# A DLRM tower on one core: GpSimd's two signals per tile at the first and the fifth eighth of the gram

## The reference

```python
e = jnp.stack([tbl_0[ids[:, 0]], ..., tbl_25[ids[:, 25]]], axis=1)
all_vecs = jnp.concatenate([dense_proj[:, None, :], sparse_embs], axis=1)
interactions = jnp.einsum('bnd,bmd->bnm', all_vecs, all_vecs)
interact_flat = interactions[:, rows, cols]
z = jnp.concatenate([dense_proj, interact_flat], axis=1)
h = jnp.concatenate([z, r_dense_proj], axis=1)
h = jnp.maximum(h @ W_top1 + b_top1, 0.0)
h = jnp.maximum(h @ W_top2 + b_top2, 0.0)
y = h @ W_top3
```

## Time and profile before

| | |
|---|---|
| median of 3 runs | 486.37 us (485.76 to 494.1) |
| the profiled execution | 485.11 us, of which the span is 483.2 |
| TensorE, matmuls | 382.4 us busy, 79% |
| TensorE, weight loads | 353.0 us, 73% |
| GpSimd | 254.9 us, 53% |
| VectorE | 230.3 us, 48% |
| ScalarE | 144.2 us, 30% |
| mean granted TensorE clock | 0.898 |

### The profile page before, as it was taken

How to read it: one execution, slowest core, us unless ns; L and a number is a source line. 1 busy time by engine, 2 the same in 40 slices (tenths; PEclk the granted TensorE clock), 3 DMA queues, 4 the chain that set the end, 5 groups by cost and what they waited for, 6 DMA issues and landing times.

```text
span 483.2 us, 14444 instructions
## 1 busy us (share of the span) xinstructions
PE 382.4 (79%) x6144; PEld 353.0 (73%) x6144; DVE 230.3 (48%) x702; ACT 144.2 (30%) x256; POOL 254.9 (53%) x260
## 2 busy tenths in 40 slices
PE   0756439686788988798799888888988899897977
PEld 0746329676777988587698887788877798786866
DVE  4779428446433375334565456446554545431110
ACT  1156013131322235024141425133324225142422
POOL 6067744655664556556666555655555766553000
PEclk9979859788898879899989988998899979897899
DMA  6998912323141422517242332313131311100000
GB/s 118 230 242 147 264 48 44 85 53 87 48 95 40 51 78 48 82 38 77 75 68 68 51 86 53 82 46 95 43 92 43 97 45 49 38 27 27 4 3 0
DMA packets 25766, 35.86 MB, mean 74 GB/s; under 512 B 6605, under 2 KB 19789, under 8 KB 25743
## 3 DMA queue, kind: packets, MB, share of 16 engines
q1 hardware_dynamic: 16399, 18.72, 20.4%
q0 software_dynamic: 8192, 16.79, 12.0%
q10 hardware_dynamic: 1152, 0.01, 0.1%
HBM read 35.49 MB, written 0.01 MB: 73 GB/s over the span
## 4 chain that ended last, share of the span: by engine, by line
PE 75%; issue 16%; DMA 5%; SPq 2%; POOL 1%; ACT 0%; DVE 0%; POOLq 0%
PE gram L424 12%; PE hid L395 11%; PE look_ps L351 7%; PE vec_act L312 7%; PE look_ps L353 7%; PE look_odd L351 6%; PE look_odd L353 6%; PE hid L402 5%; PE hid L351 4%; PE hid L353 4%; DMA raw<-tbl 3%; PE small L414 2%; DMA vecs<-tbl,ids_sb 2%; POOL vecs L295 1%; PE small L364 1%
## 5 line engine op out<-in xcount | busy, mean ns | idle before, releaser
L295 POOL DMA_INDIRECT vecs<-tbl,ids_sb x256 | 254.7, 995 | 184.5 <-issue 101.0
L572 DVE TENSOR_SCALAR onehot<-step_ids,row_no 125x256 fp32r<-125x256 int32 x640 | 187.9, 364 | 180.1 <-remote 84.4
L424 PE MATMUL gram<-vecs_T 128*27 128x26 f32 x4096 | 61.8, 201 | 52.1 <-issue 51.9
L424 PEld LDWEIGHTS gram<-vecs_T 128*27 128x27 f32 x4096 | 51.5, 113 | 64.7 <-issue 60.6
L547 ACT COPY vecs_T<-vec_act 128x512 f32<-128x512 f32 x64 | 46.1, 728 | 148.1 <-PE vec_act L312 79.3
L351 PE MATMUL look_ps<-onehot,look_hi 125*128 125x256 f32 x256 | 74.0, 319 | 6.7 <-DVE look_lo L580 4.6
L351 PE MATMUL look_odd<-onehot,look_hi 125*128 125x256 f32 x256 | 69.2, 306 | 4.3 <-DVE look_lo L580 2.7
L353 PE MATMUL look_ps<-onehot,look_lo 125*128 125x256 f32 x256 | 69.3, 301 | 2.7 <-issue 2.7
L353 PE MATMUL look_odd<-onehot,look_lo 125*128 125x256 f32 x256 | 64.4, 287 | 0.0
L351 PEld LDWEIGHTS look_ps<-onehot,look_hi 125*128 125x128 f32 x256 | 53.5, 209 | 9.0 <-DVE look_lo L580 4.8
L351 PE MATMUL hid<-onehot,look_hi 125*128 125x256 f32 x128 | 42.6, 355 | 21.0 <-DMA ident<-identity 15.6
(11 more groups left out here) (74 smaller groups left out, 293.3 us busy)
## 6 DMA issues: line engine op xcount, KB each, us to landing
step_ids<-look_ids SPq DMA_DIRECT2D x15, 640.0 KB
raw<-tbl SPq DMA_DIRECT2D x10, 448.0 KB
vecs<-tbl,ids_sb POOLq DMA_INDIRECT x256
vecs<-dense SPq DMA_DIRECT2D x16, 64.0 KB
raw<-tbl SPq DMA_DIRECT2D x10, 52.0 KB
step_ids<-look_ids SPq DMA_DIRECT2D x1, 512.0 KB
w_sb<-w SPq DMA_DIRECT2D x1, 512.0 KB
raw<-w_dense SPq DMA_DIRECT2D x1, 512.0 KB
```

The source lines that it names most:

```text
L295: nc.gpsimd.indirect_dma_start(out=vecs[j][:, 1 + k, :], out_offset=None, in_=tables[k], in_offset=bass.IndirectOffsetOnAxis(ap=ids_sb[:, ...
L424: last = nc.tensor.matmul(gram[s * QUAD:s * QUAD + VECS, g, 0:2 * FOLD], v[:, 0:VECS], v.rearrange("d (h n) -> d h n", h=2)[:, :, 0:FOLD], ...
L572: last = nc.vector.tensor_scalar(onehot[:, i % SLOTS, c, :], step_ids[a][0:LOOK_K, f - a * LOOKUPS // 2, :], row_no[0:LOOK_K, ch:ch + 1], ...
```

## The change

```diff
-PARTS = 4
+PARTS = 8
 GRAM_PARTS = tuple(QUAD * n // PARTS for n in range(PARTS + 1))
...
                     wait_for_vecs(t, j, pair)
                     gram_part(j, 0).then_inc(gram_half0, 1)
-                    gram_part(j, 1)
+                    for part in range(1, PARTS // 2):
+                        gram_part(j, part)
 
                 def gram_second(j):
-                    gram_part(j, 2).then_inc(gram_half1, 1)
-                    gram_part(j, 3).then_inc(gram_ready, 1)
+                    gram_part(j, PARTS // 2).then_inc(gram_half1, 1)
+                    for part in range(PARTS // 2 + 1, PARTS - 1):
+                        gram_part(j, part)
+                    gram_part(j, PARTS - 1).then_inc(gram_ready, 1)
```

## The result

The changed kernel takes 522.45 us, median of 4 runs (515.07 to 528.09), beside 490.24 for 4 runs of the kernel before (485.76 to 495.51): a ratio of 1.0655, interval 1.0404 to 1.0906. The prediction was 486.0 with a range of 477 to 498. The profiled execution took 520.7 us, its span is 518.8, 35.6 us longer than before. Ratios here leave disturbed executions out and so aren't always the quotient of the two medians.

What follows compares the result with a forecast made beforehand. TensorE's gram and GpSimd's gathers were taken to hold each other in a ring paced by the gathers. From the profiled 485.1 us, -7.0 and +6.7 gave 484.8, as a time 486, with a range of 477 to 498.

Steps and rivals of the forecast that it cites:

- What bounds the kernel: TensorE's gram halves and GpSimd's gather sets hold each other up; gathers set the pace, TensorE's own turn some 10.5 us.
- Term 1: Gram signals come 32 records earlier, saving 0.28 us on each of 25 turns: 7.0 us off.
- The sign that I asked for: GpSimd's pause between gather sets in the settled turns: 2.8 us where it was 3.1.
- Term 2: Start-up gram half near 83 us: signal passes while GpSimd still gathers, TensorE stands through eight more gathers; 6.7 us lost.
- sixteen gathers on end: Expected mark of a too early signal: two gather sets without pause at 1.25 us, beside a gram half over 10 us.
- With 96 left it is 0.83, still inside: Gram records left after the signal take 0.83 us, within the 1.1 us GpSimd needs to its first gather.
- In the settled turns I expect none: Where 4 to 11 gram records pass among gathers, no signal was expected to release GpSimd before its set ends.
- None reached 64: In the profile before, no releasing gram half that met gathers let 64 records through before TensorE's release.
- A: Rival: no signal passes too early in any gram half, only the 7.0 us gain is left, 479 us; chance 0.24.
- C: Rival: TensorE's own work sets the pace in most turns, so the gain is hidden, 486 us; chance 0.08.
- B: Rival: in two or more gram halves the 32nd record passes while GpSimd gathers; +9.0 us, 495 us; chance 0.30.
- D: Rival: the change doesn't do what it says; excluded by the diff, the signal being on another matmul of the same sequence.

Runs made afterwards that it cites:

- one write: Changed kernel plus one GpSimd write, which GpSimd waits for, between signal and first gather: 490.55 us on a slower chip, ratio 1.0134 to the kernel before.
- three tiny writes: Changed kernel plus three small GpSimd scratch writes between each wait and the first gather: 516.94 us on a slower chip.
- kernel before, second trace: The unchanged kernel, one more execution with its trace, on a slower chip: 501.91 us.
- three eighths: Kernel before with both signals moved later, to 96 MATMUL records into each gram half: 487.2 us on a slower chip.
- 48 or 80 records: Kernel before with both signals moved to 48 or 80 MATMUL records into the half; quicker chips: 395.92, 396.99, 396.54 us and 397.27, 399.21 us.

## Why the prediction was wrong

**What bounds the kernel.** Right. The gathers halt TensorE (without them all but four halts in the gram are gone), it goes free 2.3 to 2.7 us after the last one's start, and its own turn is 10.2 us in the mean.

**Term 1, -7.0 us.** The signal does come 0.28 us earlier, in the clean half: the first gather is 0.18 us after the last record, where it was 0.45. But the gain never shows. It holds only as long as TensorE halts inside the gram, with nothing but gram records between its release and the signal; in 14 of 27 halves that is now not so, and sets begin 14.9 us apart in the mean, where it was 13.5 and not the 12.6 to come. The sign that I asked for was there: in 12 of the 13 halves with halts GpSimd's pause is 2.5 to 3.1 us, its median 2.7. But it says nothing of the other 14, where the pause is 4.4 to 11.9.

**Term 2, the step that failed.** It priced a signal that comes too early against GpSimd's *running* set, and looked for sixteen gathers on end. There is not one such place in the changed kernel's trace. In the half at 115.41, where 34 records went through at once, I should have seen one:

```profile
115.41 0.53 PE L424 MATMUL gram<-vecs_T 128*27 128x26 f32 x34
...
121.42 1.24 PE L424 MATMUL gram<-vecs_T 128*27 128x26 f32 x84 [0.51 <-issue]
```

GpSimd's timeline there:

```profile
118.94 0.94 POOL L295 DMA_INDIRECT vecs<-tbl,ids_sb  x1 [0.30 <-issue]
122.36 0.94 POOL L295 DMA_INDIRECT vecs<-tbl,ids_sb  x1 [2.47 <-issue]
```

GpSimd waited all the same, since the signal's semaphore rose only 6.16 us after the half began, when the gathers were over: this signal, raised among gathers, was held up with the rest. The loss came from the other side of the signal, the *next* set. The sentence that failed is "With 96 left it is 0.83, still inside": I took it that a first gather behind the last gram record is harmless however near. Counted over the releasing halves (a matmul of the gram or of a layer, two records, as one instruction), TensorE gets this many instructions from the gram's last record to its first halt:

| first gather after the last gram record | instructions |
|---|---|
| -0.37 to 0 us (changed kernel) | 19 to 29 |
| 0.17 to 0.19 us (changed kernel) | 25 to 47 |
| 0.16 to 0.26 us (one write) | 40 to 53 |
| 0.32 us (three tiny writes) | 47 to 55 |
| 0.27 to 0.29 us (kernel before, second trace) | 49 to 56 |
| 0.27 to 0.45 us (kernel before) | 53 to 63, once 29, once 51 |
| 0.35 to 1.41 us (one write) | 51 to 60 |
| 0.65 to 0.74 us (three eighths) | 56 to 61 |

Left out are one set of the kernel before at -0.83 us and all sets with a long gather or a long pause near their start, 11 of 27 in the changed kernel; there it is 60 to 73 wherever the first one starts, as if it had started later. It is a slope and not a step: some 25 at 0 us, near 60 from 0.45 on, with a scatter of ten or more between. The kernel before stands near its top, and the change moved the gathers down it. Between two halves of the gram in the loop lie 56 or, every fourth time, 60 such instructions. With 57 to 60 let through the first halt falls into the gram, just; with 25 to 47 it falls ahead of it. "In the settled turns I expect none" was wrong for the same reason: I read the settled turns for what slips into the gram, not for how little lies between their first halt and the gram's start. The trace of before had it: 4 to 11 records of 128 were through the earlier trace rows, a margin of a few instructions. And it had one set that began too early. "None reached 64" is wrong for the half at 140.01: 90 of its 128 records come before its last run. TensorE's timeline, and GpSimd's:

```profile
143.50 0.51 PE L424 MATMUL gram<-vecs_T 128*27 128x26 f32 x38 [1.11 <-issue]
```

```profile
142.99 1.06 POOL L295 DMA_INDIRECT vecs<-tbl,ids_sb  x1 [2.77 <-issue]
```

The set begins 0.83 us ahead of the last gram record, only some 30 instructions get through before the first halt, and the next half comes at 159.31, 19.3 us after this one. That was the changed kernel's loss, once, in the trace that the prediction was made from.

**Rivals.** A and C (479, 486) fell with term 1. B had the right sign and the wrong mechanism and size: 9 or 17 us by slips, none of which occurred on the slower chip, where 32 came. D isn't the case. The runs of the kernel before at 494.1 us, which I read as a hint of a slip, fit the edge seen in its second trace.

**Size.** The range ended at 498 because each loss was priced as one event. What happened is a changed turn in over half of the sets, +56.8 us between the halves against -23.5 in them.

## What to carry to other kernels

Where TensorE halts while GpSimd issues gathers, ask not how much idle time a line shows but what stands between the end of the halts and the next signal; here halts that fell into the block which raises the signal were cheap, and halts ahead of it delayed the whole ring. Count how many instructions lie between the last free moment and that block, and how many get through: a margin of a few is an edge, and a signal "earlier by 0.28 us" can fall off it. And time such a change on more than one chip: it was 6.5 and 7.6% in two measurements on slower ones, and nothing on a quicker one.

## What the runs showed of the hardware

**Semaphores arrive late, not only instructions.** From the start of the gram's last matmul to the rise of `gram_ready` it is 0.22 us (median) in the kernel before, over 1 us in one of 16 tiles (in two of the 13 that its second trace has). In the changed kernel the median is 1.9 us, the longest 7.1, and 11 of 16 are over 1 us (11 again in its second trace); with three eighths 0.24 and none, with one write 0.24 and two, without gathers 0.22 and none. The chain's new 6% of "another core or an unknown queue" may go with it. But late signals aren't what the loss is made of: with the first half's signal alone at the eighth one of 16 is late, with three tiny writes two, and both traces are over 520 us long; with the second half's alone it is 13. After the half at 115.41, whose last record starts at 122.4, VectorE's timeline has

```profile
129.50 1.05 DVE L557 STREAM_TRANSPOSE gram_rows<-gram 128x832 f32<-128x832 f32 x1 [12.00 <-remote]
```

and ScalarE's

```profile
133.84 1.32 ACT L550 COPY vecs_T<-vec_act 128x512 f32<-128x512 f32 x2 [17.32 <-remote]
```

the first 7 us after the gram was done. "Remote" is what the profile says where it finds no instruction that ended near the semaphore's rise. Copies of the transposes are late in both kernels; in the changed one it reaches `gram_ready` as well.

**A clock step follows the halts.** After the half at 190.85 to 197.4, which had halts, the changed kernel's window reads

```profile
197.80:200.30 2.50, 2.50 (x13) 2.50 (x13) 0.00 (x0) 0.00 (x0) 1.89 (x3) 0.50 0.36 60
```

a granted clock of 0.50, the 1.2 GHz level, with look-ups 0.21 us apart in place of 0.12. This is part of the 7 us that the lower clock makes of the loss.

**Plain loads didn't halt TensorE like that.** In one execution on the quicker chip 16 of them a tile, 0.55 us each, leave 23 of 27 halves at the 1.1 us of an undisturbed one; in the changed kernel's trace there, with gathers, it is 10. On a slower chip they weren't tried. The Trainium skill, "Runtime: NRT & Kernel Launch", section "Instruction fetch mechanics", has refills of instructions mostly hidden. With gathers the traces of the slower chips show matmul starts 0.7 and 1.4 us apart where the halts are, in code that runs without halts when no gathers are issued, except for the four longer ones named above. So whatever the refills cost, gathers decide it here; whether the four are refills, no run shows.

**Chips differ.** The same kernel takes 397 or 492 us. Without gathers it is 377.6 and 383.9, so nearly all of the difference comes with the gathers. It includes the clock: the granted clock of the kernel before is 0.96 to 0.98 on the quicker chips and 0.88 to 0.91 on the slower, and 0.97 on both kinds without gathers.

**What stays open.** What it is that runs dry or fills up while GpSimd gathers, so that both instructions and messages of TensorE stop, and why a few tenths of a microsecond of distance change how much gets through. Every execution here was recorded, so whether recording has a part in it can't be told. Why chips differ wasn't tried, nor was 48 or 80 records on a slower one.
